# Routing the first three tiles inside the first half of the cross attention of a decoder layer

## What is computed

```python
scores = jax.nn.softmax(xt @ Wg.T, axis=-1)            # 16 experts in 4 groups
group_scores = scores.reshape(T, G, E // G).max(axis=-1)
gidx = jax.lax.top_k(group_scores, TOPK_G)[1]          # 2 groups
topi = jax.lax.top_k(masked, TOPK)[1]                  # 4 experts in them
h = silu(xt @ W1[e]) * (xt @ W3[e]);  expert_out = h @ W2[e]
y = sum over the 4 chosen experts of score * expert_out
z = (silu(xt @ Ws1.T) * (xt @ Ws3.T)) @ Ws2.T          # shared part, every token
x = x + y + z
```

## Time and profile before

| what | us |
|---|---|
| median of 3 runs | 714.1 (712.3 to 716.24) |
| the profiled execution | 711.57 |
| its span, first to last instruction | 710.3 |
| TensorE busy in it | 591.7 (83%) |
| VectorE busy | 393.3 (55%) |
| ScalarE busy | 249.9 (35%) |
| GpSimd busy | 222.4 (31%) |
| first half of the cross attention | 315.57 to 409.60 |
| second half of it | 409.60 to 509.50 |
| shared tiles, routing | to 557.50 |
| blocks | to 692 |

### The profile page before, as it was taken

One profiled execution on the slowest core, in us unless ns is written; L12 is line 12 of the kernel. 1 busy time (PEld: TensorE's weight loads), 2 busy tenths in 40 slices (PEclk: granted clock), 3 DMA queues, 4 the chain that ended last, 5 costly groups with the idle time before them and its releaser, 6 DMA issues.

```text
span 710.3 us, 10711 instructions
## 1 busy us (share of the span) xinstructions
PE 591.7 (83%) x3751; PEld 483.7 (68%) x3751; DVE 393.3 (55%) x921; ACT 249.9 (35%) x516; POOL 222.4 (31%) x179
## 2 busy tenths in 40 slices
PE   5889989999998899999999979274679768888960
PEld 5779978988877775666666557263568657777850
DVE  4376476274555487656664668642356464444436
ACT  1344455354643501121211164112123465444440
POOL 3525230120001023234333423128155383334340
PEclk9899999999999999999999999667667999999995
DMA  8999430040999793000000050002242552333307
GB/s 257 253 232 229 103 148 1 2 162 26 267 214 203 226 211 77 1 1 0 1 1 0 1 198 1 1 22 89 95 143 61 177 171 78 90 90 91 95 21 295
DMA packets 41106, 76.94 MB, mean 108 GB/s; under 512 B 4823, under 2 KB 27999, under 8 KB 40800
## 3 DMA queue, kind: packets, MB, share of 16 engines
q1 hardware_dynamic: 19616, 49.65, 24.1%
q10 hardware_dynamic: 17648, 18.18, 12.0%
q0 software_dynamic: 3792, 8.43, 3.3%
HBM read 66.77 MB, written 28.48 MB: 134 GB/s over the span
## 4 chain that ended last, share of the span: by engine, by line
PE 49%; DVE 19%; DMA 10%; issue 10%; POOL 5%; ACT 4%; ACTq 1%; SPq 1%; POOLq 0%; DVEq 0%
PE psum L660 5%; PE psum L678 5%; PE psum L823 5%; DMA sclB<-in_scl 4%; PE psum L594 4%; PE psum L581 4%; PE psum L529 4%; PE psum L542 3%; DVE tt L1216 3%; DMA parts_of_tokens<-yb,xg 2%; PE psum L753 2%; POOL rows_of_experts L1585 2%; DVE sm L1152 2%; PE psum L722 2%; DVE Pb L1180 2%
## 5 line engine op out<-in xcount | busy, mean ns | idle before, releaser
L1216 DVE TENSOR_TENSOR tt<-psum,tab 128x512 f32<-128x512 f32 x96 | 60.4, 683 | 24.1 <-PE psum L660 23.3
L1591 POOL DMA_INDIRECT parts_of_tokens<-yb,xg x47 | 47.9, 1019 | 77.4 <-ACT yb L1049 69.5
L823 PE MATMUL psum<-EW,xgh 128*128 x188 | 58.1, 351 | 10.0 <-issue 9.5
L1557 POOL TENSOR_TENSOR rp<-tt,tt 128x512 f32<-128x512 f32 x24 | 30.7, 1281 | 94.6 <-DVE tt L1216 94.6
L529 PE MATMUL psum<-xTh,W 128*128 128x512 f32 x128 | 53.7, 420 | 6.5 <-DVE W L1116 4.2
L678 PE MATMUL psum<-rp,Mb 128*128 128x512 f32 x128 | 57.8, 596 | 1.1 <-POOL rp L1560 0.8
L529 PE MATMUL psum<-xTl,W 128*128 128x512 f32 x128 | 52.4, 409 | 0.0
L1186 DVE TENSOR_TENSOR OTl<-psum,OTh 128x512 fp32r<-128x512 f32 x32 | 22.1, 692 | 54.6 <-ACT OTh L922 54.6
L1442 DVE TENSOR_TENSOR xgl<-psum,xgh 128x256 fp32r<-128x256 f32 x47 | 19.9, 424 | 58.1 <-ACT xgh L1031 48.9
L823 PEld LDWEIGHTS psum<-EW,xgh 128*128 128x128 f32 x188 | 34.5, 190 | 17.7 <-issue 17.3
L660 PE MATMUL psum<-xTh,Ah 128*128 128x512 f32 x96 | 42.5, 442 | 2.0 <-DVE tt L1216 2.0
(11 more groups left out here) (223 smaller groups left out, 1597.3 us busy)
## 6 DMA issues: line engine op xcount, KB each, us to landing
rows_of_experts<-in_empty ACTq DMA_DIRECT2D x7, 2064.0 KB, 19.5
exr<-in_ex SPq DMA_DIRECT2D x16, 608.0 KB, 5.9
xg<-rows_of_experts SPq DMA_DIRECT2D x47, 129.0 KB
raw<-in_codes SPq DMA_DIRECT2D x4, 1024.0 KB, 17.4
sclB<-in_scl SPq DMA_DIRECT2D x16, 256.0 KB, 11.7
yv<-parts_of_tokens SPq DMA_DIRECT2D x8, 512.0 KB, 7.0
rows_of_experts<-in_empty ACTq DMA_DIRECT2D x1, 2193.0 KB, 23.8
raw<-in_codes SPq DMA_DIRECT2D x4, 512.0 KB, 16.4
```

What stands on the lines that cost most here:

```text
L823: mm = pe.matmul(ap[:, 0:352], xp[b % 2][:, 128 * kt:128 * kt + 128], EW[:, bass.ds(weights[b] + (o + 352 * kt), 352)], start=(k == 0), st ...
L1216: return tt_(b3(tt[n][:, :], 64), b3(src, 64), tab[:, j % 3, n, :].unsqueeze(1).to_broadcast([128, 8, 64]), ALU.mult)
L1557: tt_(o[:, 0, :], tt[0][:, :], tt[1][:, :], ALU.subtract).then_inc(s_rp_lo, 1)
L1591: nc.gpsimd.indirect_dma_start(out=parts_of, out_offset=to, in_=yb[b % 4][:, :], in_offset=None, bounds_check=4 * 1024 - 1, oob_is_err=Fal ...
```

## The change

The order of the list, the groups, the experts by engine and the silu of the later tiles change:

```diff
-BY_POOL = (0, 1, 2, 3, 4, 5, 6, 7, 8, 10, 12, 14)
-GROUPS = ((0, 4), (4, 2), (6, 1), (7, 1))
+BY_POOL = (2, 3, 6, 8, 10, 12, 14)
+GROUPS = ((0, 3), (3, 3), (6, 2))
+BY_TANH = 2

-PLANS = (((0, 0, 0, 2, 0, 3, 0),
+PLANS = (((0, 0, 0, 2, 0, 2, 0),
           (0, 0, 0, 2, 0, 2, 1),
-          (0, 1, 0, 2, 0, 1, 1),
-          (0, 1, 0, 2, 0, 1, 2)),)
+          (0, 1, 0, 1, 0, 1, 1),
+          (1, 2, 1, 1)),)
...
@@ cross_order
+            if t % 4 == 3 and n == 0:
+                yield ("logits", 0)
+            if t % 4 == 3 and n == 2:
+                yield ("route", 0, 0)
+            if t % 4 == 3 and n == 3:
+                yield ("route", 0, 1)
+                yield from next(fill, [])
+                yield ("route", 0, 2)
...
@@ block_order
-        if 2 <= s and BEFORE + s - 2 < NE:
-            step += [("expert", BEFORE + s - 2)]
+        if s + 6 < NE:
+            step += [("expert", s + 6)]
...
@@ hidden, on ScalarE
-                    act(sl[t % 2][:, u, :], ps.of("h", t, u)[:, 0:176], ACT.Tanh, scale=0.5).then_inc(s_sl, 1)
+                    act(sl[t % 2][:, u, :], ps.of("h", t, u)[:, 0:176], ACT.Tanh if t < BY_TANH else ACT.Silu,
+                        scale=0.5 if t < BY_TANH else 1.0).then_inc(s_sl, 1)
...
@@ mix, on VectorE: the first of the two operations only for t < BY_TANH
```

More of the change, by code:

```diff
@@ L56, in second_half @@
 def second_half():
[L59 to L67, removed]
+    yield from [("cross_turn", 3), ("cross_scores", 4), ("cross_exp", 4), ("rank", 0), ("cross_values", 3),
+                ("cross_norm", 4, 0), ("cross_norm", 4, 1), ("copies", 0), ("cross_scores", 5), ("cross_exp", 5),
+                ("dispatch", 0)]
     for t in range(4, 8):
-        yield from [("cross_turn", t), ("cross_out", t - 1), ("norm", 2, (t - 1,))]
+        yield ("cross_turn", t)
+        if t == 7:
+            yield from [("logits", 1), ("route", 1, 0)]
         if t < 7:
[L71 to L78, removed]
+            yield from [("cross_norm", t + 1, 0), ("cross_norm", t + 1, 1)]
+        yield from [("cross_out", t - 1), ("norm", 2, (t - 1,))]
+        if t == 4:
+            yield ("scatter", 0)
+        if t == 5:
+            yield from [("scatter", 1), ("scatter", 2)]
+        if t == 7:
+            yield ("route", 1, 1)
+        yield from [("center", 2, (t - 1,)), ("cross_values", t)]
         if t < 6:
@@ L83, in second_half @@
         yield ("norm_turn", 2, t - 1)
-        yield from [w for w in late[t] if t < 7 or w != r1[3]]
+        if t == 4:
+            yield from [("copies", 1), ("copies", 2)]
+        if t == 5:
+            yield ("copies", 3)
+        if t == 6:
+            yield from [("hidden", 0), ("mix", 0), ("expert", 0), ("copies", 4)]
+        if t == 7:
+            yield from [("hidden", 1), ("route", 1, 2), ("copies", 5)]
     yield from [("cross_out", 7), ("norm", 2, (7,))]
 def last_routes():
-    r1, r2, r3 = (routing(n) for n in (1, 2, 3))
@@ L91, in last_routes @@
[L91 to L102, removed]
+    yield from [("turn_hidden", 0), ("rank", 1), ("mix", 1), ("center", 2, (7,)), ("dispatch", 1), ("turn_low", 0)]
@@ new lines, in last_routes @@
+    yield from [("down", 0), ("norm_turn", 2, 7), ("scatter", 3), ("scatter", 4), ("turn_hidden", 1), ("logits", 2)]
+    yield from [("route", 2, 0), ("turn_low", 1), ("add_shared", 0), ("copies", 6), ("hidden", 2), ("down", 1)]
+    yield from [("route", 2, 1), ("add_shared", 1), ("hidden", 3), ("route", 2, 2), ("rank", 2), ("mix", 2)]
+    yield from [("dispatch", 2), ("scatter", 5), ("scatter", 6), ("copies", 7), ("scatter", 7), ("turn_hidden", 2)]
+    yield from [("turn_low", 2), ("mix", 3), ("hidden", 4), ("turn_hidden", 3), ("down", 2), ("table", 0)]
@@ new lines, in last_routes @@
+    yield from [("turn_low", 3), ("mix", 4), ("add_shared", 2), ("expert", 1), ("hidden", 5), ("down", 3)]
+    yield from [("table", 1), ("turn_hidden", 4), ("mix", 5), ("turn_low", 4), ("add_shared", 3), ("expert", 2)]
+    for t in (6, 7):
+        yield from [("hidden", t), ("down", t - 2), ("turn_hidden", t - 1), ("mix", t), ("turn_low", t - 1),
+                    ("add_shared", t - 2), ("expert", t - 3)]
+    yield from [("down", 6), ("turn_hidden", 7), ("turn_low", 7), ("add_shared", 6), ("down", 7), ("expert", 5),
+                ("add_shared", 7)]
@@ L984, in route @@
                     sc_.wait_ge(*ps.emptied("lg", n))
-                    act(ex_l[:, 0:some, :], ex_l[:, 0:some, :], ACT.Exp).then_inc(s_rexp, 1)
+                    part_ = work[n > 0].ex_l[:, 0:some, :]
+                    act(part_, part_, ACT.Exp).then_inc(s_rexp, 1)
             def split13():
```

125 lines of the change are left out of this document (73 added, 52 removed).

## The result

| | before | after |
|---|---|---|
| median, both measured together | 713.2 us (711.17 to 716.24) | 672.31 us (670.98 to 675.82) |
| ratio, 95% interval | | 0.9431 (0.938 to 0.9482) |
| the profiled execution | 711.57 | 670.98 (forecast 675.4) |
| its span | 710.3 | 669.7 |

The forecast was 678 us within 661 to 700. One execution each of a_route_late, a_splits_early, a_plan_drain and a_mended was slow (over 1.5% above that kernel's fastest), and a_mended's is the one that was profiled.

A forecast was written before the change was run, and what follows sets the result against it. TensorE bounds it: busy through the first half, then waiting for cum and xh and slowed by a low clock. 711.57 - 38.2 (sooner block start) + 2.0 (blocks) = 675.4 profiled, 678 at the median; range 661 to 700.

The forecast's parts named there:

- the likeliest case: The forecast of 678 us for the whole kernel, from 672 to 684, given a chance of 0.50.
- both long waits: TensorE's idle times before: 10.60 us for cum ending at 457.06, 11.30 for xh ending at 498.60; claimed to be removed.
- 1, first half: Up to cross_values(3): logits(0) for three tiles adds 2.1 us, waits of latent(1,6) and cross_turn(2) 2.2; together +4.3.
- the walk: Following the engines' queues with the durations of the trace, which gave waits and tile periods without low clock.
- The contention: First half: GpSimd's rp operations slowing VectorE; taken as 0 (ends 0 and 2.6 us), by the skill's rule 1.3 to 2.5.
- 2, four periods: Tiles 4 to 7: four periods of 12.1 us, 48.4 (ends 43 and 56), to cross_values(7) at 466.5.
- 3, up to cross_out(7): From cross_values(7) to the end of cross_out(7): 10.3 us, ending at 476.8 where before it was 509.3.
- 4, shared tiles: From cross_out(7) to down(7): 27.1 us of work, 9.9 of waits, 5.6 for low clock; 42.6, ending at 519.4.
- 5, blocks: Block stage: three more experts split +1.5, two GpSimd splits +1.8, table load -1.3; taken +2, ends -1 and +8.
- Silu: Shared tiles: 0.33 us per half tile off VectorE, at most 2 us on the path, counted within the waits.
- the full walk: Rival: TensorE never long at low clock, periods of 10.8 us, no 5.6 us in shared tiles; 667 us, chance 0.15.
- GpSimd's queue: Rival: dispatch(1) at 492 puts scatters, landing and fetch at 523, setting the blocks' start; 681.5 us, chance 0.10.

The follow-up runs named there:

- a_route_late: The kernel after with group 0 routed in the second half again, where it was before; 686.75 us, ratio 0.9581.
- a_splits_early: The kernel after with the experts' weight splits where and by whom they were before, twelve on GpSimd; 679.38 us, ratio 0.9427.
- a_plan_drain: The kernel after with the old latent plan for tiles 0 and 2 and route(0,0) right behind logits(0); 682.86 us, run again 683.46.
- a_mended: The kernel after with route(0,0) right behind logits(0), scatter(2) one tile later, the split of expert 4 behind down(7); 667.89 us, ratio 0.9352.
- a_old_plan: The kernel after with the latents' steps of tiles 0 and 2 where they were before; 681.87 us, ratio 0.9576.
- the two runs: The kernel after with tanh in all shared tiles, 673.93 us; the kernel before with silu for tiles 4 to 7, 713.6 us.
- b_scatter_late: The kernel before with the scatters of tiles 2 and 3 behind the norm of tile 6; 704.13 us, ratio 0.9815.
- a_drain_early: The kernel after with route(0,0) moved right behind logits(0); 674.82 us, ratio 0.9485.
- b_filler: The kernel before with 90 and 100 transposes that nobody reads on TensorE in its two long waits; 711.28 us, ratio 0.9978.

## Why the prediction was right

The time was 5.7 us below the forecast and just inside the range of the likeliest case, 672 to 684. What the forecast named as the way to it happened: both long waits went, with them most of the low clock. That the sum came so close is in part luck, since errors of both signs cancel: against the profiled execution (670.98, forecast 675.4), the start took 2.8 us more and the first half 2.3 more than forecast, the periods 3.6, the shared tiles 2.3 and the blocks 3.5 less. By its steps:

**1, first half.** Forecast +4.3 up to cross_values(3), measured +6.6 there, less the start's 2.8 (+6.4 up to latent(1,7)). logits(0) took 2.3 us (393.90 to 396.22) for 2.1, and cross_turn(2) waited 0.57 + 0.93 for the 1.4 of the walk. The wait of latent(1,6) didn't come, and the one of 0.76 that was there before went. Missed was a resource: I followed the queues through tiles and semaphores of data, and not through the PSUM bank that logits(0) shares with the rotations, 2.34 us. And the longer wait ahead of cross_values(1), 0.7, belongs to the plan. a_old_plan shows that both can be avoided. rank(0) was hidden, as forecast.

**The contention.** The rule of the Trainium skill (SBUF — State Buffer, "SBUF: two separate sides") that I had put beside the sum holds here: a normalising multiply took 1.07 us at 402.07, beside GpSimd's rp operations (400.09 to 402.59), and 0.69 at 424.57; and sca, with two inputs in SBUF, took 1.09 at 413.21, beside an rp from 412.98 to 414.25, where the reciprocal at 413.00, with one, took 0.18. gsel itself ran free, 0.18 us, as in my walk. What stood is 0.4 + 0.9 us, the low end of the 1.3 to 2.5 I gave for the rule, and TensorE didn't wait for either. It did wait for a third that I hadn't looked for, in tile 2: a multiply at 373.52 took 1.07 us beside an rp from 372.76 to 374.03, and cross_turn(2) waited 0.57 us for it.

**2, four periods.** Forecast 48.4 from 12.1 each, measured 44.8 (9.80, 11.10, 8.85, 15.05); the walk at full clock gave 43.1. The term was too large by 3.6 us because I had put the one period that before had without a route in place of the walk's mean. Where it came out is chance too: with the same waits, the stretch these periods are in took 57.6 to 61.8 us, by the clock. rst of tile 5 waited behind a scatter, as forecast; with four of the issues moved (a_mended) TensorE's wait behind it is 1.2 us shorter.

**3, up to cross_out(7).** 10.3 us forecast, 10.3 measured (468.0 to 478.25).

**4, shared tiles.** Forecast 42.6, measured 40.3. The wait for turn_low(0) was 3.27 us for 4.0, the one at rank(2) 0.54 for 1.7, and the clock was low from 481 to 491 only, where down(0) took 2.29 us for 1.08 and hidden(2) 3.4 for 1.93. That is some 4 us of extra duration for the 5.6 I took.

**5, blocks.** Forecast +2, measured -1.5, which is less than this stretch varies (149.3 to 152.6 us in the four kernels with the old order). No cost of the three more experts shows: GpSimd's returns have a mean of 1.04 us for 1.02, and the block stage of a_splits_early, without those experts, is no shorter. The upper end, one more late fetch, didn't come. The split ahead of the last down did show once: it took 3.15 us at 513.57, twice its 1.41 at 517.44, beside GpSimd's double split from 509.89, and down(7) waited 2.5 us for the gTl behind it.

**Silu** was put at 2 us at most on the path; the two runs say 0.4 and nothing.

**The rivals.** The result lies halfway between the forecast and the full walk, 667: two of the four periods ran at a clock of 1.00, the others at 0.83 and 0.89, and the periods' sum came out near the walk's. GpSimd's queue didn't set the end: the last scatter ended at 509.9 (forecast 508) and down(7) at 518.6 (519.4), so the cover was 8.7 us less landing and fetch.

The prediction named removed waits as the cause of all 38.2 us. The runs divide the stretch more finely: 14.7 us for routing early, 7.3 for moving the splits, 2.2 for both, and 16.2 for what is left, each from single profiles that the clock moves by up to 4 us. What is left is the smaller groups and the order of the scatters; b_scatter_late alone takes 8.8 us off, but off the kernel before, so it can't be subtracted from the 16.2. No run undoes the groups by themselves, so their share isn't shown. The prediction also put some 7 us of the wait for cum on splits beside the route. In the late route with groups of three, that wait is 8.49 us with the splits there and 6.03 without, so they make 2.5 us of it; with groups of four no run tells.

## What to carry to other kernels

Look for the short operation that many wait for behind a long one that nobody waits for: one rst of 0.6 us behind sixteen DMA issues held TensorE for 11.3 us, and moving eight of the issues brought 8.8 us. When a chain is moved under work that fills an engine, list the buffers it takes there beside its data; the bank that logits(0) left full held TensorE for 2.34 us, as long as its own matmuls (2.32). And after an edit, compare stretches between fixed instructions rather than whole times: the start of this kernel varies by more than most single edits bring. Read the granted clock beside each stretch, and compare idle times: the same order took 4 us more or less by the clock alone.

## What the runs showed of the hardware

- How long TensorE stays at 1.2 GHz isn't told by the length of the wait before it. In the kernel after, it waited 3.26 us ahead of 458.15 and 3.27 ahead of 483.10. Behind the first it was back at full clock by 462, behind the second it stood at 0.50 for 10 us, busy all the while. In a_drain_early TensorE waited 3.27 us at the place of the first (ahead of 457.34), and the clock stayed at 1.00. Nor does it take a long wait: in b_filler the clock was 0.50 from 501.7 on, though TensorE had waited no more than 0.21 us at a time since the filler of 487.67. Windows of the kernel after, then one of a_drain_early and one of b_filler, with the columns of the first fence:

```profile
456.00:462.00 6.00, 3.85 (x18) 3.86 (x19) 1.58 (x4) 0.83 (x3) 1.48 (x2) 0.72 0.12 44
462.00:468.00 6.00, 6.00 (x41) 5.59 (x40) 2.43 (x5) 3.38 (x6) 0.00 (x0) 1.00 0.00 0
...
483.00:490.90 7.90, 7.80 (x34) 7.80 (x35) 2.35 (x11) 2.45 (x5) 5.91 (x6) 0.50 0.62 194
```

```profile
456.00:462.00 6.00, 4.66 (x38) 4.67 (x38) 3.08 (x7) 2.97 (x6) 0.66 (x2) 1.00 0.06 22
```

```profile
501.70:505.00 3.30, 3.30 (x13) 3.12 (x12) 0.00 (x0) 0.63 (x2) 0.00 (x0) 0.50 0.00 0
```

- A VectorE operation of 0.2 us with two SBUF inputs can take 1.1 beside GpSimd work, and a DMA issue on GpSimd 2.18 instead of 0.97 beside a weight split on VectorE (503.86 and 503.78).
- The same code up to the first cross_scores took between 315.6 and 327.4 us in fourteen profiles, more than any stretch behind it varied where its code was the same and no late signals stood in it.
- Signals of TensorE that others see 3.8 us late, in four runs of three kernels, at the same places of the program. It makes 11 to 13 us of difference, and no row of the profile says why.
